# A recurrent attention block with a gated MLP on one core: the first score block issued earlier, the last output pieces and loads moved

## What is computed

```
q, k = rope(xn @ wq.T), rope(xn @ wk.T);  v = xn @ wv.T
per chunk of 64 tokens (lam per head):
  scores  = (q k^T) * exp(-lam * (i - j)) for i >= j
  o       = scores v + (q * exp(-lam * (i + 1))) state
  state   = exp(-64 lam) * state + (k * exp(-lam * (63 - j)))^T v
out = x + (o @ wo.T) * g
```

## Time and profile before

| | |
|---|---|
| profiled execution | 924.73 us |
| its span, first to last instruction | 922.9 us |
| median of three runs | 925.86 us |
| VectorE / ScalarE / GpSimd busy | 68% / 46% / 39% of the span |
| granted TensorE clock, mean | 0.998 of full speed |
| bytes moved | 138.55 MB, 150 GB/s over the span |
| one common step of the attention | 36.4 us |

### The profile page before, as it was taken

The page is one execution under the profiler, slowest core; times in us unless marked ns, Lnnn a source line. Parts: engine busy times, 40 slices in busy tenths (PEclk is TensorE's granted clock), DMA queues, the critical chain, the costliest instruction groups (busy, mean ns, idle before and its releaser), DMA issues.

```text
span 922.9 us, 12461 instructions
## 1 busy us (share of the span) xinstructions
PE 899.3 (97%) x4128; PEld 738.6 (80%) x4128; DVE 627.0 (68%) x915; ACT 421.7 (46%) x709; POOL 362.2 (39%) x267
## 2 busy tenths in 40 slices
PE   5999999999999999999999999999999999999996
PEld 4888888888888878888888888878888878878776
DVE  7778653586553346666687766776866678779686
ACT  3643533443432555444455344464554454543531
POOL 1011112121122565535535545455455364554541
PEclk9999999999999999999999999999999999999999
DMA  6792213469650542331443504333423145356352
GB/s 209 226 368 91 103 46 125 174 241 326 251 205 7 199 153 110 137 121 61 145 143 119 199 23 160 135 117 136 158 81 136 38 167 205 105 181 227 115 182 81
DMA packets 51403, 138.55 MB, mean 150 GB/s; under 512 B 4256, under 2 KB 25888, under 8 KB 45984
## 3 DMA queue, kind: packets, MB, share of 16 engines
q1 hardware_dynamic: 51360, 138.00, 42.5%
HBM read 96.04 MB, written 41.94 MB: 150 GB/s over the span
## 4 chain that ended last, share of the span: by engine, by line
PE 43%; issue 30%; POOL 19%; DVE 4%; ACT 1%; DMA 1%; POOLq 0%; SPq 0%; DVEq 0%; ACTq 0%
PE bank L1210 43%; POOL d_r L1168 10%; POOL rot L1177 9%; PE bank L1257 1%; DVE d_sb L1001 1%; DMA stage<-in_x_nat 1%; DMA tail_sb<-mlp_gate 1%; DVE q_r L994 0%; DVE d_sb L1046 0%; DVE rot L987 0%; ACT d_r L682 0%; ACT gout L538 0%; DVE rot L988 0%; ACT rot L662 0%; ACT st_r L671 0%
## 5 line engine op out<-in xcount | busy, mean ns | idle before, releaser
L1210 PE MATMUL bank<-xn,aw 128*128 128x512 f32 x960 | 228.6, 389 | 0.0
L1177 POOL TENSOR_TENSOR rot<-rot 128x512 f32<-128x512 f32 x80 | 127.8, 1597 | 236.6 <-DVE rot L988 236.6
L1210 PEld LDWEIGHTS bank<-xn,aw 128*128 128x128 f32 x960 | 179.2, 188 | 36.6
L1168 POOL TENSOR_TENSOR d_r<-d_sb,d_r 128x512 fp32r<-128x512 f32 x128 | 166.6, 1329 | 51.9 <-ACT d_r L682 51.9
L1210 PE MATMUL bank<-o_r,ow 128*128 128x512 f32 (+1 forms) x816 | 186.4, 379 | 0.0
L1210 PE MATMUL bank<-xn,gu_w 128*128 128x512 f32 x768 | 179.9, 389 | 0.0
L1210 PEld LDWEIGHTS bank<-xn,gu_w 128*128 128x128 f32 x768 | 144.2, 188 | 30.1
L1210 PEld LDWEIGHTS bank<-o_r,ow 128*128 128x128 f32 x816 | 145.7, 188 | 27.5
L682 ACT CAST d_r<-d_sb 128x512 fp32r<-128x512 f32 x128 | 78.9, 621 | 100.4 <-DVE d_sb L1046 67.1
L987 DVE TENSOR_TENSOR rot<-bank,rope 128x512 f32<-128x512 f32 x80 | 55.2, 690 | 98.0 <-ACT rot L662 97.8
L661 ACT COPY rot<-bank 64x512 f32<-64x512 f32 x80 | 46.7, 584 | 145.9 <-PE bank L1210 145.4
(11 more groups left out here) (75 smaller groups left out, 946.1 us busy)
## 6 DMA issues: line engine op xcount, KB each, us to landing
xn<-xn_split SPq DMA_DIRECT2D x15, 2048.0 KB, 7.8
v_decayed<-vd_split SPq DMA_DIRECT2D x32, 512.0 KB, 3.4
vd_r<-v_decayed SPq DMA_DIRECT2D x16, 1024.0 KB, 6.9
v_r<-v_split SPq DMA_DIRECT2D x16, 512.0 KB, 5.8
wst<-in_mlp_w SPq DMA_DIRECT2D x10, 768.0 KB, 5.3
xn_split<-xn SPq DMA_DIRECT2D x3, 2048.0 KB, 10.8
stage<-in_attn_w SPq DMA_DIRECT2D x4, 1280.0 KB, 6.1
stage<-in_x_nat SPq DMA_DIRECT2D x16, 256.0 KB, 4.7
```

The lines of the kernel that those rows point to most:

```text
L1168: pool.tensor_tensor(d_r[:, slot(e), 1, :], d_sb[:, slot(e), :], d_r[:, slot(e), 0, :].bitcast(F32), ALU.subtract).then_inc(d_lo, 1)
L1177: pool.tensor_tensor(rot1[:, r % RRING, :], rot1[:, r % RRING, :], rot2[:, r % RRING, :], ALU.add).then_inc(qk_sum, 1)
L1210: last = pe.matmul(dst, a, b, start=start and x == 0, stop=stop and x == len(pairs) - 1)
```

## The change

- The elements are renumbered: q elements are e = 0 and 2 (EL_Q), score block 0 is e = 1, blocks 1 to 5 stay e = 3 to 7 (EL_B). ScalarE and POOL take block 0 between the two q elements. PE still uses both q elements first; USED gives the count at which it has used one.
- PE issues score block 0 of step n + 1 behind projection 4 and ahead of output projection 2 (except in step 0).
- VectorE decays it in round 4, between the decay of the third q head and the accumulation of piece 2.
- ScalarE rounds the state behind element 2, as before it did behind element 1. In step 0 it rounds gates and state ahead of elements 1 and 2.
- In the last group piece 2 is finished with piece 3 in the next step, behind the output tiles; in the last step these four instructions stand among the decay blocks and output splits (`last_step`).
- SP issues all four tail loads (8 transfers) behind the store of piece 1. The loads that refill pieces 1 to 3 of the earlier sequences stay behind their stores, which now come later.
- The last output projection has 6 tiles: second halves of pieces 0 and 1, whole pieces 2 and 3, first halves of 0 and 1. It has the same products.

```diff
+EL_Q = [0, 2]
+EL_B = [1, 3, 4, 5, 6, 7]
+USED = [EL_Q.index(e) if e in EL_Q else SC + EL_B.index(e) for e in range(NEL)]
...
-        TAIL = [(half, u) for half in (1, 0) for u in range(KT)]
+        TAIL = [(0, slice(HALF, S)), (1, slice(HALF, S)), (2, slice(0, S)), (3, slice(0, S)), (0, slice(0, HALF)), (1, slice(0, HALF))]
...
                     if final and b < NB - 1:
-                        if b == NB - 2:
-                            load_tail(0)
                         for u in range(1, KT):
                             store_fin(b, u)
                             if b < NB - 2:
                                 load_fin(b + 1, u - 1)
-                            else:
-                                load_tail(u)
+                            elif u == 1:
+                                for tail_u in range(KT):
+                                    load_tail(tail_u)
...
-                decayed_round(n, 0)
+                decayed_round(n, EL_Q[0])
                 qk_round(n, QK - 1)
-                decayed_round(n, 1)
-                for other in beside.get("state", ()):
-                    other()
-                st_round(n)
+                if is_first(n):
+                    for other in beside.get("state", ()):
+                        other()
+                    st_round(n)
+                decayed_round(n, EL_B[0])
+                decayed_round(n, EL_Q[1])
+                if not is_first(n):
+                    st_round(n)
...
+            def last_step(n, b):
+                decay_block(n, HEAD)
+                finish_gate(n - 1, b - 1, KT - 2)
+                decay_block(n, HEAD + 1)
+                finish_gate(n - 1, b - 1, KT - 1)
+                decay_block(n, HEAD + 2)
+                finish_add(b - 1, KT - 2)
+                o_rest(n, 0)
+                o_rest(n, 1)
+                finish_add(b - 1, KT - 1)
+                o_rest(n, 2)
+                o_rest(n, 3)
+                for k in range(len(TAIL)):
+                    tail_piece(k)
...
-                    finish(n - 1, b - 1, KT - 1)
+                    for u in (KT - 2, KT - 1):
+                        finish_gate(n - 1, b - 1, u)
+                        finish_add(b - 1, u)
...
+                after = {r: [lambda u=r - 2: collect(u)] for r in (2, 3, 4)}
+                after[QK - 1] = [lambda: decay_block(n + 1, 0)] + after[QK - 1]
...
-                for e in range(SC):
+                for e in range(EL_Q[1] + 1):
                     decayed_rest(n, e)
...
                 projections(n + 1, g_edge, beside={2: [first_out], 3: [lambda: out_projection(n, g, 1)],
-                                                   4: [lambda: out_projection(n, g, 2)]})
+                                                   4: [lambda: scores(n + 1, 0), lambda: out_projection(n, g, 2)]})
                 state(n + 1)
                 out_projection(n, g, KT - 1)
-                for t in range(HEAD):
+                for t in range(1, HEAD):
                     scores(n + 1, t)
                 inter(n + 1)
```

More of the change, by code:

```diff
@@ L473, in last_stores @@
             def last_stores():
-                for k, (half, u) in enumerate(TAIL):
+                for k, (u, cols) in enumerate(TAIL):
                     sp.wait_ge(tail_d, k + 1)
-                    sp.dma_start(out[u, :, bass.ts((NB - 1) * 2 + half, HALF)],
-                                 tail_in(u)[:, 0, bass.ts(half, HALF)]).then_inc(tail_stored, 16)
+                    sp.dma_start(out[u, :, (NB - 1) * S + cols.start:(NB - 1) * S + cols.stop],
+                                 tail_in(u)[:, 0, cols]).then_inc(tail_stored, 16)
             load_xn(0, 1)
@@ L750, in _ @@
                             "state": [lambda: gates(NB - 1)]})
-            for t in range(HEAD):
-                decayed_round(0, SC + t)
+            for t in range(1, HEAD):
+                decayed_round(0, EL_B[t])
             run_steps(act, step)
@@ L1070, in tail_piece @@
             def tail_piece(k):
-                half, u = TAIL[k]
-                b, cols = NB - 1, bass.ts(half, HALF)
+                u, cols = TAIL[k]
+                b, width = NB - 1, cols.stop - cols.start
                 x, gate = tail_in(u)[:, 0, cols], tail_in(u)[:, 1, cols]
                 dve.wait_ge(tail_out, k + 1)
-                dve.tensor_tensor(acc[:, b, u, cols], tail_ps[k // KT][u][:, 0:HALF], acc[:, b, u, cols],
+                dve.tensor_tensor(acc[:, b, u, cols], tail_ps[k][:, 0:width], acc[:, b, u, cols],
                                   ALU.add).then_inc(tail_acc, 1)
@@ L1086, in collect @@
                     accumulate(n, g, b, u)
-                    if final and u < KT - 1:
-                        finish(n, b, u)
+                    if final and u < KT - 2:
+                        finish_gate(n, b, u)
+                        finish_add(b, u)
+                if last:
+                    last_step(n, b)
+                    return
                 for t in range(HEAD, NBL):
@@ L1097, in step @@
                     aw_split_lo(g + 1, 1)
-                elif not last:
+                else:
                     rotate(n + 1, 0)
@@ L1106, in step @@
                     rotate(n + 1, 0)
[L1107 to L1118, removed]
+                beside = {}
+                if edge:
+                    beside = {r: [lambda t=t: aw_split_lo(g + 1, t) for t in ts] for r, ts in ((0, (3, 4)),)}
+                if start:
+                    beside = {r: [lambda h=h: ow_split_lo(g, h) for h in hs] for r, hs in ((0, (0, 1, 2)), (1, (3,)))}
+                after = {r: [lambda u=r - 2: collect(u)] for r in (2, 3, 4)}
+                after[QK - 1] = [lambda: decay_block(n + 1, 0)] + after[QK - 1]
+                projections(n + 1, g + 1 if edge else g, g + 1 if edge else None, beside, after)
                 st_rest(n + 1)
-                for t in range(HEAD):
+                for t in range(1, HEAD):
                     decay_block(n + 1, t)
@@ L1189, in step @@
                 projections(n + 1)
-                for t in range(HEAD):
-                    decayed_rest(n + 1, SC + t)
+                for t in range(1, HEAD):
+                    decayed_rest(n + 1, EL_B[t])
             first = (NB - 1) * MT
@@ L1199, in _ @@
                             QK: [lambda: fuse_rest(first + 10), lambda: fuse_rest(first + 11)]})
-            for t in range(HEAD):
-                decayed_rest(0, SC + t)
+            for t in range(1, HEAD):
+                decayed_rest(0, EL_B[t])
             run_steps(pool, step)
@@ L1386, in inter @@
                 for x in range(QD):
-                    pe.wait_ge(d_lo, n * NEL + x + 1)
+                    pe.wait_ge(d_lo, n * NEL + EL_Q[x] + 1)
                     tile = inter_ps[x][:].rearrange("p (h c) -> p h c", h=2)
                     for h in range(2):
-                        last = products(tile[:, h, :], [(st_r[:, a, 2 * x + h, :], d_r[:, slot(x), c, bass.ts(h, HALF)])
+                        last = products(tile[:, h, :], [(st_r[:, a, 2 * x + h, :], d_r[:, slot(EL_Q[x]), c, bass.ts(h, HALF)])
                                                         for a, c in SPLIT], start=(h == 0), stop=False)
@@ L1434, in last_out_projection @@
                 pe.wait_ge(acc_d, n * KT + KT)
[L1435 to L1442, removed]
+                for k, (u, cols) in enumerate(TAIL):
+                    if k == 0:
+                        pe.wait_ge(o_lo, n * NOT + 2)
+                    elif k == 2:
+                        pe.wait_ge(o_lo, n * NOT + NOT)
+                    products(tail_ps[k][:, 0:cols.stop - cols.start], [(ow[:, a, h, bass.ts(u, P)], o_r[:, c, h, cols])
+                                                                       for h in range(HG) for a, c in SPLIT]).then_inc(tail_out, 1)
             def out_projection(n, g, u):
```

33 lines of the change are left out of this document (19 added, 14 removed).

## The result

The changed kernel took 935.96 us (median of 4 runs, 935.36 to 937.2) against 926.02 us before in the same comparison; the ratio is 1.0108, 95% interval 1.009 to 1.0125. It is slower by 1.1%. The forecast was 934.8. The medians differ by 9.9 us; the two profiled executions (935.36 and 924.73) differ by 10.6, and their spans by 10.7.

A forecast was written before the change was run, and what follows sets the result against it. TensorE was taken as the bound, busy 97% of the span. Terms +10.1 + 2.5 - 0.8 - 2.9 = +8.9 us gave 933.6 profiled, 934.8 as median; own range 931 to 938 (0.70), full range 917.5 to 938.

The forecast's parts named there:

- The lock: In a common step, POOL's rest of score block 0 goes ahead of the fourth q decay, which ends 1.20 us later.
- The common transitions: The 12 transitions into steps 1 to 12: each next projection starts 0.84 us later, +10.1 us in all.
- the q decay slips in before POOL: Rival: the fourth q decay goes before POOL and ends only 0.10 us later than before; sum -7.3, time 918.5; chance 0.25.
- Step 0: POOL takes block 0 before the second q element, so the state product's second half waits; +2.5 us, bounds 0.5 and 3.2.
- The last group: Its first two transitions become common ones as piece 2's finish moves into the next step; -0.8 us together.
- the tail: At the end, earlier loads remove the 2.70 us wait for a gate piece; -2.9 us, bounds -4 and -1.5.
- I let the output projection start at 904.25: After the third transition of the last group, the output projection starts at 904.25 instead of 904.51.
- The load of the decayed v: L404 in the last transition goes out some 2 us later, still in time; costs nothing, without this cover up to 2.

The follow-up runs named there:

- the exchange: The changed kernel with VectorE's decay of score block 0 placed behind the accumulation of output piece 2 instead of ahead of it; 919.62 us.
- the halves: The changed kernel with POOL's rest of block 0's element made in two 256-column instructions instead of one of 512, except in step 0; 928.28 us.
- the double: The changed kernel with POOL's rest of block 0's element made twice, the second after the first is through, except in step 0; 935.93 us.

## Why the prediction was right

**The lock.** The step that carried the forecast was that POOL arrives inside L994 and ahead of the fourth q decay, and that the q decay then ends 1.20 us later. In the profile after it takes 1.51 us and inter is 1.12 us later behind the scores; POOL was 0.32 us ahead where 0.38 was forecast. The exchange by 0.6 us, the halves and the double all behave as a lock held per instruction would have it. The Trainium skill, page "SBUF — State Buffer", section "Who interferes with whom", states an exclusive lock that the first to issue holds; the runs agree. They add who comes next: in the kernel with the halves VectorE, which waits, goes ahead of POOL's second half, which is ready.

**The number.** 934.8 was forecast and 935.96 measured, inside the narrow range of 931 to 938. The full range, 917.5 to 938, reached down over the rival and would have held it too, so the narrow one is the test. The sum of the changes was +8.9 us and came out as +10.7 in the profiled executions; the medians, which differ by 9.9, hide part of this.

**The common transitions** were +10.25 us for +10.1. The size is partly luck: ten of them grew by 0.67 to 0.84, 0.77 in the mean, a little less than my 0.84. The two in steps 7 and 11, at the end of a group, grew by 1.3, for a second meeting at the same lock (L887) that I had not looked for.

**The rival** "the q decay slips in before POOL" is a kernel now: the exchange gave 919.62 where it said 918.5, with step 0 at some 4.2 instead of 2.5. That a few tenths of a us of arrival time decide was right: POOL 0.31 to 0.39 us ahead of the q decay's issue is the dear case, 0.21 to 0.29 behind it the cheap one. Where between them it turns, no run shows; 0.4 us was the forecast's distance to it.

**Step 0** was mis-sized: "+2.5 us" was 4.20. The end of the gap was right (347.55 forecast, 347.54 measured). What failed is "ends about 348.3, and the projection comes at 348.3 + 4.15": the 4.15 us are a price at full clock, and behind a gap of 2.84 us PE ran most of this stretch at half of it: from 348.36, 5.74 us were needed instead of 4.15. In the common transitions PE's idleness of 1.14 us had no such effect.

**The last group and the tail.** -0.8 was -1.23. The second transition gave -0.50, as forecast (9.10 less 9.58). The first gave -0.73 instead of -0.3: my 9.4 for it was right (9.44), but "these transitions become common ones" was not quite, as inter waits only 0.86 us there (step 13; steps 1 and 4 are alike with 0.87) and not 1.14. "I let the output projection start at 904.25" failed by 0.3: the gate multiplications among the last decays hold the lock against POOL, and both last v products wait. I had named this lock and given it no number of its own. The load of the decayed v was late by 2.9 us rather than 2 and cost nothing. From the output projection to the end it took 15.84 us for 15.75.

What stays open is how the last transition would run without any finish work in it (it was not tried), and why step 0 costs a further us in some executions, as told in the last section.

## What to carry to other kernels

Where VectorE and GpSimd work on the same chain, look at who is issued first, not at how busy they are: a VectorE instruction with two SBUF inputs behind a GpSimd one costs that one's whole remaining length, here 1.1 us, and 15 times that, with step 0's 4, turned a gain of 10 us into a loss of 10. Put instructions that read PSUM into the gap while GpSimd works, and let the short instruction on the critical path be issued before the other engine's input is ready; an exchange of two neighbours can do it. When an element of a queue is moved, ask on every engine that it passes what it now stands in front of, and do it once more for the steps that are written out on their own.

## What the runs showed of the hardware that was not expected

PE's granted clock fell to 0.50 at a wait of 2.84 us in step 0, and three groups of matmuls took 1.24 to 1.48 us; behind waits of 0.86 to 1.22 us in the later steps the matmuls took their usual 0.84 to 0.86 us, and the clock was at 1.00.

The price of this one wait is not fixed. The kernels with the halves and with the double have the same step 0 and the same wait of 2.84 us, but there the clock fell while PE was still waiting, and the second half of inter took 1.65 us instead of 0.98. From it to the next projection it was 7.61 and 7.40 us, against 6.56 in the change and 6.54 in the exchange. What decides between the two is not shown. The rows of the halves:

```profile
348.65 1.65 PE L1247 MATMUL bank<-d_r,st_r 128*128 128x256 f32 x6 [2.84 <-POOL d_r L1205]
```

```profile
347.00:348.00 1.00, 0.00 (x0) 0.00 (x0) 0.00 (x0) 0.59 (x2) 1.00 (x2) 0.78 0.87 338
```

And the lock passes to the waiting engine: in the kernel with the halves, VectorE waits for the first of two POOL instructions in a row and goes ahead of the second in all 15 steps.
